# Splitting a matrix stream over two DMA queues: odd chunks of adj issued by ScalarE, its arithmetic given to VectorE and GpSimd

## What is computed

```python
def reference(x, adj, L0_gnn_u):             # x (8192, 64), adj (8192, 8192), u (8192, 64), float32
    keep = (u >= 0.1).astype(x.dtype)
    x_drop = x * keep / (1.0 - 0.1)
    y = x + jnp.matmul(adj, x_drop)
    m = jnp.mean(y, axis=-1, keepdims=True)
    v = jnp.var(y, axis=-1, keepdims=True)
    return (y - m) / jnp.sqrt(v + 1e-5)
```

## Time and profile before

| | us |
|---|---|
| median of 3 runs | 664.59 (664.55 to 664.62) |
| span of the profiled execution | 662.8 |
| TensorE busy | 502.1 |
| VectorE busy | 45.5 |
| ScalarE busy | 26.4 |
| GpSimd busy | 0.7 |

### The profile page before, as it was taken

The page is one execution under the profiler, slowest core; times in us unless marked ns, Lnnn a source line. Parts: engine busy times, 40 slices in busy tenths (PEclk is TensorE's granted clock), DMA queues, the critical chain, the costliest instruction groups (busy, mean ns, idle before and its releaser), DMA issues.

```text
span 662.8 us, 6659 instructions
## 1 busy us (share of the span) xinstructions
PE 502.1 (76%) x2592; PEld 158.6 (24%) x2592; DVE 45.5 (7%) x223; ACT 26.4 (4%) x41; POOL 0.7 (0%) x7
## 2 busy tenths in 40 slices
PE   1777777777877778778777777777777877878786
PEld 0112121121211222211222112221122221244565
DVE  1210001000200002000020000200002000010111
ACT  0000010000100001000020000200002000100000
POOL 0000000000000000000000000000000000000000
PEclk9999999999999999999999999999999999999999
DMA  8999999999999999999999999999999999999995
GB/s 341 419 421 423 420 421 424 421 422 423 421 422 423 422 422 424 422 421 423 422 421 424 422 422 423 422 423 422 422 422 423 421 422 423 422 420 422 420 421 220
DMA packets 39898, 274.89 MB, mean 415 GB/s; under 512 B 4432, under 2 KB 4816, under 8 KB 7248
## 3 DMA queue, kind: packets, MB, share of 16 engines
q1 hardware_dynamic: 37296, 268.45, 97.4%
q10 hardware_dynamic: 2592, 6.29, 2.5%
HBM read 272.63 MB, written 2.10 MB: 414 GB/s over the span
## 4 chain that ended last, share of the span: by engine, by line
DMA 70%; SPq 23%; PE 5%; issue 2%; DVE 0%; ACT 0%; DVEq 0%
DMA adj_ring<-adj_chunks 70%; SPq L116 21%; PE acc L172 5%; SPq L111 2%; SPq L115 0%; DVE u_nat L249 0%; DVE stats L227 0%; PE back L185 0%; ACT std L146 0%; DVE summed L221 0%; ACT acc_sb L143 0%; DVE rstd L246 0%; DVE gap L233 0%; DVE mean L241 0%; DVE squares L243 0%
## 5 line engine op out<-in xcount | busy, mean ns | idle before, releaser
L172 PE MATMUL acc<-adj_ring,x_drop 128*64 128x512 f32 (+2 forms) x2560 | 496.2, 518 | 151.7 <-DMA adj_ring<-adj_chunks 136.9
L172 PEld LDWEIGHTS acc<-adj_ring,x_drop 128*64 128x64 f32 x2560 | 155.4, 136 | 487.4 <-DMA adj_ring<-adj_chunks 312.8
L221 DVE TENSOR_TENSOR summed<-back,x_nat 128x256 f32<-128x256 f32 (+1 forms) x17 | 6.3, 404 | 581.6 <-PE back L185 581.6
L143 ACT COPY acc_sb<-acc 128x256 f32<-128x256 f32 (+1 forms) x17 | 5.4, 362 | 593.2 <-PE acc L172 593.2
L249 DVE TENSOR_SCALAR u_nat<-summed,mean,rstd 128x64 f32 (+1 forms) x64 | 15.2, 308 | 1.0
L143 ACT ACT_TABLE_LOAD x7 | 9.0, 1283 | 23.8 <-DVE u_nat L249 18.6
L185 PE MATMUL back<-identity,acc_sb 128*128 128x128 f32 x32 | 6.1, 302 | 4.5 <-ACT acc_sb L143 4.5
L227 DVE BATCH_NORM_STATS2 stats<-summed 128x6 f32<-128x64 f32 x64 | 9.0, 210 | 0.1
L146 ACT ACT_TABLE_LOAD x7 | 9.0, 1283 | 0.1
L259 DVE SCALAR_TENSOR_TENSOR x_drop<-u_nat,x_nat 128x1024 f32<-128x1024 f32 x4 | 4.9, 1226 | 28.5 <-DMA u_nat<-u 28.5
L185 PEld LDWEIGHTS back<-identity,acc_sb 128*128 128x128 f32 x32 | 3.3, 140 | 12.1 <-ACT acc_sb L143 11.6
(11 more groups left out here) (5 smaller groups left out, 0.5 us busy)
## 6 DMA issues: line engine op xcount, KB each, us to landing
adj_ring<-adj_chunks SPq DMA_DIRECT2D x255, 1024.0 KB, 27.3
x_nat<-x ACTq DMA_DIRECT2D x4, 512.0 KB, 17.0
u_nat<-u ACTq DMA_DIRECT2D x4, 512.0 KB, 20.3
out<-u_nat ACTq DMA_DIRECT2D x7, 256.0 KB, 7.1
adj_ring<-adj_chunks SPq DMA_DIRECT2D x4, 256.0 KB, 24.4
out<-u_nat ACTq DMA_DIRECT2D x1, 128.0 KB, 8.0
out<-u_nat ACTq DMA_DIRECT2D x2, 64.0 KB, 4.8
```

Of the source, the lines that this page charges most:

```text
L143: nc.scalar.copy(acc_sb[:, b * width:(b + 1) * width], acc[:, b * width:(b + 1) * width]).then_inc(acc_copied, 1)
L172: last = nc.tensor.matmul(acc[h * D:(h + 1) * D, 0:width], x_drop[:, t * D:(t + 1) * D], adj_ring[:, slot, at:at + width], start=(t == 0), ...
L221: nc.vector.tensor_tensor(summed[:, b * width:(b + 1) * width], back[b][:, 0:width], x_nat[:, bass.ds(row * D + b * width, width)], ALU.ad ...
```

## The change

The even chunks are issued by SP and the odd ones by ScalarE. ScalarE issues chunks 1, 3, 5 and 7 between the pieces of x and u, one behind each piece; then 9, 11, 13, 15, and then in turns of 16 the odd slots. The last chunk, 255, is odd: its four quarters go over ScalarE's queue. ScalarE does nothing else any more.

The copies of the accumulator are made by VectorE, at the head of its group. The square root and the reciprocal become a scale-and-add on VectorE, (squares / 64) + eps, and a power with exponent -0.5 on GpSimd, which VectorE waits for. `eps` and `std` are gone; `var_eps` and `minus_half` are new.

The stores are issued by SP. That of a full group is issued behind the load of chunk 22 of the next group (`STORE_AT`); that of the last full group behind chunk 22 of the 32 chunks of the short groups; the three short ones after all loads. SP also waits for all stores at the end.

```diff
         @block.sync
         def _(sp):
-            for s in range(SLOTS):
-                sp.dma_start(adj_ring[:, s, :], adj[s]).then_inc(chunk_loaded[s], 16)
-            with sp.Fori(1, CHUNKS // SLOTS - 1) as turn:
-                for s in range(SLOTS):
-                    sp.wait_ge(chunk_used, (turn - 1) * SLOTS + s + 1)
-                    sp.dma_start(adj_ring[:, s, :], adj[turn * SLOTS + s]).then_inc(chunk_loaded[s], 16)
...
+            def store(n, row, rows):
+                sp.wait_ge(normed_ready, n + 1)
+                sp.dma_start(out_rows[:, bass.ds(row * D, rows * D)],
+                             normed[:, bass.ds(row * D, rows * D)]).then_inc(out_stored, 16)
+
+            for s in range(0, SLOTS, 2):
+                sp.dma_start(adj_ring[:, s, :], adj[s]).then_inc(chunk_loaded[s], 16)
+            for k in range(SLOTS, NC, 2):
+                sp.wait_ge(chunk_used, k - SLOTS + 1)
+                sp.dma_start(adj_ring[:, k % SLOTS, :], adj[k]).then_inc(chunk_loaded[k % SLOTS], 16)
+            with sp.Fori(1, FULL) as g:
+                for k in range(0, NC, 2):
+                    sp.wait_ge(chunk_used, g * NC + k - SLOTS + 1)
+                    sp.dma_start(adj_ring[:, k % SLOTS, :], adj[g * NC + k]).then_inc(chunk_loaded[k % SLOTS], 16)
+                    if k == STORE_AT:
+                        store(g - 1, (g - 1) * R, R)
...
+            for n, (row, rows, _) in enumerate(SHORT_GROUPS):
+                store(FULL + n, row, rows)
+            sp.wait_ge(out_stored, 16 * (FULL + len(SHORT)))
 
         @block.gpsimd
...
+            for n, rows in enumerate([R] * FULL + SHORT):
+                pool.wait_ge(var_ready, n + 1)
+                nc.gpsimd.tensor_tensor(rstd[:, 0:rows], var_eps[:, 0:rows], minus_half[:, 0:rows],
+                                        ALU.pow).then_inc(rstd_ready, 1)
 
         @block.scalar
...
             for i in range(PIECES):
                 cols = slice(i * PIECE, (i + 1) * PIECE)
                 act.dma_start(x_nat[:, cols], x_rows[:, cols]).then_inc(x_loaded[i], 16)
                 act.dma_start(u_nat[:, cols], u_rows[:, cols]).then_inc(x_loaded[i], 16)
...
+                act.dma_start(adj_ring[:, 2 * i + 1, :], adj[2 * i + 1]).then_inc(chunk_loaded[2 * i + 1], 16)
+            for s in range(2 * PIECES + 1, SLOTS, 2):
+                act.dma_start(adj_ring[:, s, :], adj[s]).then_inc(chunk_loaded[s], 16)
+            with act.Fori(1, CHUNKS // SLOTS - 1) as turn:
+                for s in range(1, SLOTS, 2):
+                    act.wait_ge(chunk_used, (turn - 1) * SLOTS + s + 1)
+                    act.dma_start(adj_ring[:, s, :], adj[turn * SLOTS + s]).then_inc(chunk_loaded[s], 16)
...
         @block.vector
         def _(dve):
-            def group(n, row, rows, parts, done):
+            def group(n, row, rows, chunks, parts, done):
+                dve.wait_ge(chunk_used, chunks)
+                across = rows * P // 2 // parts
+                for b in range(parts):
+                    nc.vector.tensor_copy(acc_sb[:, b * across:(b + 1) * across],
+                                          acc[:, b * across:(b + 1) * across]).then_inc(acc_copied, 1)
...
-                dve.wait_ge(std_ready, n + 1)
-                nc.vector.reciprocal(rstd[:, 0:rows], std[:, 0:rows]).then_inc(rstd_ready, 1)
+                dve.wait_ge(squares_ready, n + 1)
+                nc.vector.tensor_scalar(var_eps[:, 0:rows], squares[:, 0:rows], 1.0 / D, EPS,
+                                        ALU.mult, ALU.add).then_inc(var_ready, 1)
                 dve.wait_ge(rstd_ready, n + 1)
```

More of the change, by code:

```diff
@@ L22 @@
 LAST_PARTS = 4
+STORE_AT = 22
 PIECES = 4
@@ L42, in build @@
     ALU = mybir.AluOpType
-    ACT = mybir.ActivationFunctionType
     x_rows = x.rearrange("(p t) d -> p (t d)", p=P)
@@ L63, in build @@
         identity = sb("identity", [P, P])
-        eps = sb("eps", [P, 1])
         acc_sb = sb("acc_sb", [P, HALF])
@@ L73, in build @@
         mean = sb("mean", [P, R])
-        std = sb("std", [P, R])
+        var_eps = sb("var_eps", [P, R])
         rstd = sb("rstd", [P, R])
+        minus_half = sb("minus_half", [P, R])
         acc = ctx.enter_context(nc.psum_tensor("acc", [P, HALF], fp32))
@@ L88, in build @@
         drop_ready = sem("drop_ready")
+        half_ready = sem("half_ready")
         zeros_ready = sem("zeros_ready")
@@ L98, in build @@
         squares_ready = sem("squares_ready")
-        eps_ready = sem("eps_ready")
-        std_ready = sem("std_ready")
+        var_ready = sem("var_ready")
         rstd_ready = sem("rstd_ready")
@@ L127, in _ @@
+            for k in range(0, NC, 2):
+                sp.wait_ge(chunk_used, FULL * NC + k - SLOTS + 1)
+                sp.dma_start(adj_ring[:, k % SLOTS, :], adj[FULL * NC + k]).then_inc(chunk_loaded[k % SLOTS], 16)
+                if k == STORE_AT:
+                    store(FULL - 1, (FULL - 1) * R, R)
+            for n, (row, rows, _) in enumerate(SHORT_GROUPS):
+                store(FULL + n, row, rows)
+            sp.wait_ge(out_stored, 16 * (FULL + len(SHORT)))
         @block.gpsimd
@@ L133, in _ @@
                                     base=0, pattern=[[-1, P]], channel_multiplier=1).then_inc(identity_ready, 1)
+            nc.gpsimd.memset(minus_half[:], -0.5).then_inc(half_ready, 1)
+            pool.wait_ge(half_ready, 1)
+            for n, rows in enumerate([R] * FULL + SHORT):
+                pool.wait_ge(var_ready, n + 1)
+                nc.gpsimd.tensor_tensor(rstd[:, 0:rows], var_eps[:, 0:rows], minus_half[:, 0:rows],
+                                        ALU.pow).then_inc(rstd_ready, 1)
         @block.scalar
         def _(act):
[L137 to L152, removed]
             for i in range(PIECES):
@@ L157, in _ @@
                 act.dma_start(u_nat[:, cols], u_rows[:, cols]).then_inc(x_loaded[i], 16)
[L158 to L163, removed]
+                act.dma_start(adj_ring[:, 2 * i + 1, :], adj[2 * i + 1]).then_inc(chunk_loaded[2 * i + 1], 16)
[5 more added lines that the diff above has]
+                    act.dma_start(adj_ring[:, s, :], adj[turn * SLOTS + s]).then_inc(chunk_loaded[s], 16)
+            first = CHUNKS - SLOTS
+            for s in range(1, SLOTS - 1, 2):
+                act.wait_ge(chunk_used, first - SLOTS + s + 1)
+                act.dma_start(adj_ring[:, s, :], adj[first + s]).then_inc(chunk_loaded[s], 16)
+            act.wait_ge(chunk_used, CHUNKS - SLOTS)
+            for i in range(LAST_PARTS):
+                cols = slice(i * SLOT // LAST_PARTS, (i + 1) * SLOT // LAST_PARTS)
+                act.dma_start(adj_ring[:, SLOTS - 1, cols], adj[CHUNKS - 1][:, cols]).then_inc(last_loaded[i], 16)
         @block.tensor
@@ L265, in _ @@
             with dve.Fori(0, FULL) as g:
-                group(g, g * R, R, 2, g * 2)
-            for n, (row, rows, _) in enumerate(SHORT_GROUPS):
-                group(FULL + n, row, rows, 1, 2 * FULL + n)
+                group(g, g * R, R, (g + 1) * NC, 2, g * 2)
+            for n, (row, rows, chunk) in enumerate(SHORT_GROUPS):
+                group(FULL + n, row, rows, chunk + rows * NC // R, 1, 2 * FULL + n)
 def kernel(x, adj, L0_gnn_u):
```

1 line of the change is left out of this document (removed).

## The result

The changed kernel takes 669.35 us (median of 4 runs, 667.93 to 669.51), the kernel before 664.61 us beside it: a ratio of 1.0066, 95% interval 1.0054 to 1.0079. It is 4.74 us slower. I had forecast 667.7 us, with a range of 665.0 to 671.2.

What follows compares the result with a forecast made beforehand. The prediction took the DMA stream of adj chunks to bound the kernel. Its terms 0 + 2.5 + 0 + 0.02 + 0.6 = 3.1 us, added to 664.59, gave 667.7 us, range 665.0 to 671.2.

Steps and rivals of the forecast that it cites:

- Part 1, the rate: Stream of adj chunks: two queues neither speed nor slow the transfer; 0, bounds minus 12 to plus 12 ns a chunk.
- faster: Rival, 0.07: two queues hide each transfer's end (semaphore packets) behind the other's data; 661.3 us at 25 ns a chunk.
- Part 2, the order: Arrival order: chunks land in pairs, streams about level at the end, chunk 254 lands with 255's last part or later; +2.5 us.
- a lead is left over: Rival, 0.18: one stream finishes early, the other's last chunks come alone; 669.1 us for one, 670.5 two, 673.3 four.
- Parts 3 and 4: Waits and issues moved between SP and ScalarE: cost 0; accumulator copy on VectorE instead of ScalarE: +0.02 us on the tail.
- Part 5, the power: Tail's square root replaced by VectorE's scale-and-add and GpSimd's power: 1.15 us instead of 0.56, so +0.6, bounds 0 and +1.4.
- Twice the select: GpSimd's power on the tail, taken as twice its affine select of 0.29 us: 0.6 us.
- one after the other: Rival, 0.17: even stream one chunk ahead at the end, or queues alternate in whole transfers; chunk 254 lands as now; 665.2 us.

Runs made afterwards that it cites:

- level queues: Changed kernel with each full group's store halved over both queues, x's pieces on SP's queue and u's on ScalarE's: 665.22 us beside 664.58.
- The arithmetic alone: Kernel before, all transfers as they were, with only the copy on VectorE and the root as a power on GpSimd: 665.09 us beside 664.58.

## Why the prediction was right, and where it was off

**Part 1, the rate: right.** I took 0 for two queues from the earlier trace rows and bounded it by 12 ns a chunk. The slices read the same before and after, and with level queues the time is that of one queue and the same arithmetic to 0.13 us. The end of each transfer that *faster* would have hidden shows as packets under 512 B: 4432 in 277 transfers, 16 for each, before and after. No gain came of them. That they are the semaphore's was my reading; no run shows it.

**Part 2, the order: the cause was right, its price was not.** Pairs every 4.97 us, an odd chunk 12.5 us after another at the start, and one chunk lost for each store are in the trace. So is the early lead of five or six chunks: from 0 to 60 us SP's queue moved 12.58 MB and ScalarE's 11.33, 4.19 of them x and u, a lead of 5.2 chunks. The step that failed is "at the end the streams are about level ... So chunk 254 lands with the last part of 255, or after it", priced at 2.5 us; it measured 4.2. Five or six less seven is a lead of one or two on the odd side and not level, and 2.0 was measured. I also looked at the last pair alone, while the last store stands directly before the last four even chunks: it makes chunk 248 late, and the backlog is eight chunks. 2.9 us of the 4.2 is that backlog (646.35 + 14.20 - 657.66); 1.3 us is the clock after the wait, for which my sum had no term at the end, though I had seen eight slow matmuls at the start in the earlier trace rows and used them only for a rival. (What made those eight slow isn't shown: the granted clock reads 1.00 there.) And the 2.5 us themselves were wrong: a level pair costs 0.1 to 0.3, since three quarters of chunk 255 come behind chunk 254. That the sum came within 1.7 us is in part luck: it priced a state that costs next to nothing and left out the lead and the clock.

The rival *a lead is left over* names what happened, and it had 0.18. It should have had more than the forecast: a cost that is smallest when two streams are exactly level and grows on both sides shouldn't be taken at its lowest point. Its 669.1 us for one chunk is near to what was measured, but by luck too: it stands on the same 2.5 us, prices a left-over chunk at 1.4 where the rows give 1.07 (TensorE does two chunks in 3.55 us and not in 3.9 when it doesn't wait), and the lead was two chunks.

**Parts 3 and 4: right in what they cost.** SP waited for chunk_used before each load, as it must with full slots, but the stores of full groups never waited for VectorE, and the rate stayed as it was. Not all of ScalarE's issues took 0.36 us: the longest, at 33.17 us, took 8.41, and the queues moved 421 GB/s beside it. VectorE's copy took 0.29 us, as its nearest row had it.

**Part 5, the power: nearly.** +0.6 forecast, 0.45 measured (squares to normalization 1.01 us instead of 0.56). The scale-and-add took 0.17. The power took 0.70 and not 0.6, but GpSimd began it 0.08 us after the scale-and-add and not 0.23, and VectorE went on 0.03 us after the power and not 0.1. Twice the select was an estimate without a row of a power. The runs show now that a power is more work an element: 0.70 us for 2 columns, and (1.64 - 0.70) / 6 = 0.16 us for each of six more, where the select took 0.29 for 128 columns. The table loads of before were two a turn, 14 of 1.28 us on ScalarE; the changed kernel has none. The arithmetic alone measured 0.5.

The rival *one after the other* had the queues alternate in whole transfers. That fits no run here in which two queues were full: such turns would land the two of a pair 2.485 us apart, and TensorE, which needs 1.94 us for a chunk, would wait between them. It did both chunks, sixteen matmuls in the full groups, without a wait in every pair of the rows above. And spreading the transfers over two issuing engines brought no bandwidth in any of the six kernels with two queues: 422 GB/s from 60 to 600 us, as with one.

## What to carry to other kernels

This stream is bound by the DMA engines (97.4% of their time went to its queue), and a second issuing queue changed only the order of arrival. Every transfer here, whole chunk, quarter, piece or store, was 144 packets (20016 on q10 for 139 transfers, 19872 on q1 for 138). So an extra transfer on one of the queues took turns like a whole chunk, though a store's rows are 2 KiB and a chunk's 8, and set that queue's chunks back by one: seven chunks in seven stores. If two queues are wanted, give them equal numbers of packets, keep stores away from the last loads, and look at the last unbroken stretch of the consumer: its length in chunks is the backlog, and at the wait just before it, which cost 1.3 us again through the clock (0.50 after 3.54 us of waiting; 1.00 after 0.45 us with the store moved). The rate itself moved only with longer runs in each partition: 422 to 431 GB/s, 11.6 us, by three constants. The chunk of 4 MiB gave some of it back at the end, most of the missing 1.5 us.

## What was not expected of the hardware

A 256 KB store, 0.1% of the bytes, cost 3.0 us where it stood before the last even chunks. The low clock (0.50) after the wait that it made cost 1.3 us (15.51 instead of 14.20 us for the same 256 matmuls). GpSimd's power took longer with more columns: 0.70 us for 128x2, 1.01 for 128x4 and 1.64 for 128x8. One execution of the changed kernel took 667.93 us and the others 669.3 to 669.5; whether that is another lead at the end or another moment of the clock wasn't tried.
